# A three-layer graph attention kernel in fp32: gamma and beta of the first norm folded into W1, early loads in another order and place, the hidden split read from zt, and E turned through another PSUM bank

## The reference

```python
h = relu(layernorm(x))                          # no gamma, beta
for l in range(3):
    si = h @ attn_w[l, :d];  sj = h @ attn_w[l, d:]
    s = leaky_relu(si[:, :, None] + sj[:, None, :] + attn_b[l], 0.2)
    attn = softmax(where(adj + eye > 0, s, -inf))
    y = layernorm(h + attn @ h) * g1[l] + beta1[l]
    ff = gelu(y @ W1[l] + b1[l]) @ W2[l] + b2[l]    # W1: 256 x 1024
    h = layernorm(y + ff) * g2[l] + beta2[l]
return x + h
```

## Time and profile before

| what | value |
|---|---|
| median of 3 runs | 1242.52 us (1242.37 to 1242.93) |
| profiled execution, its own time | 1241.6 us |
| its span, first to last instruction | 1239.8 us |
| busy: PE, DVE, ACT, POOL | 1196.4, 1075.9, 920.0, 677.4 us |
| chain that ended last | PE 95%, DVE 3%, SP's queue 1%, DMA 1% |
| mean granted TensorE clock | 0.998 |
| POOL L487 (h_gamma), 128x512 | 96 times, mean 1298 ns |

### The profile page before, as it was taken

How to read it: one execution, slowest core, us unless ns; L and a number is a source line. 1 busy time by engine, 2 the same in 40 slices (tenths; PEclk the granted TensorE clock), 3 DMA queues, 4 the chain that set the end, 5 groups by cost and what they waited for, 6 DMA issues and landing times.

```text
span 1239.8 us, 23072 instructions
## 1 busy us (share of the span) xinstructions
PE 1196.4 (97%) x7509; PEld 1082.8 (87%) x7509; DVE 1075.9 (87%) x3568; ACT 920.0 (74%) x1754; POOL 677.4 (55%) x648
## 2 busy tenths in 40 slices
PE   2699999999999999999999999999999999999997
PEld 1589999998999999999999999999999999999996
DVE  5899889999998888899998888899989988888865
ACT  3786887678877776778778767777887777677752
POOL 1354455456755554456666545554666455545564
PEclk9999999999999999999999999999999999999999
DMA  7122322233332111222432122122432321122221
GB/s 256 38 77 73 99 70 60 77 94 112 103 103 88 50 44 52 85 71 85 129 114 92 43 59 70 44 69 78 125 115 80 100 60 43 44 69 61 78 89 48
DMA packets 109620, 100.57 MB, mean 81 GB/s; under 512 B 12952, under 2 KB 95932, under 8 KB 109500
## 3 DMA queue, kind: packets, MB, share of 16 engines
q1 hardware_dynamic: 109500, 99.10, 26.3%
HBM read 66.47 MB, written 32.60 MB: 80 GB/s over the span
## 4 chain that ended last, share of the span: by engine, by line
PE 95%; DVE 3%; SPq 1%; DMA 1%; issue 0%; POOL 0%; ACT 0%; DVEq 0%; POOLq 0%
PE acc L1073 44%; PE hbank L1058 42%; PE mix L1087 7%; PE mix L1112 2%; DMA adji<-in_adj_dram 1%; DVE xs L757 0%; DVE junk L694 0%; DVE st L603 0%; DVE st L764 0%; SPq L313 0%; PE util L1104 0%; SPq L332 0%; DVE sc L729 0%; POOL rstd L467 0%; DVE hid_lo L615 0%
## 5 line engine op out<-in xcount | busy, mean ns | idle before, releaser
L1073 PE MATMUL acc<-w2hi,hid_hi 128*128 128x256 f32 x1536 | 442.2, 288 | 0.0
L1073 PE MATMUL acc<-w2hi,hid_lo 128*128 128x256 f32 x1536 | 434.5, 283 | 0.0
L1073 PE MATMUL acc<-w2lo,hid_hi 128*128 128x256 f32 x1536 | 434.4, 283 | 0.0
L912 ACT ACTIVATE hbank<-hbank,vec 128x512 f32<-128x512 f32 x384 | 255.4, 665 | 178.1 <-PE hbank L1058 167.0
L1058 PE MATMUL hbank<-ht_hi,w1hi 128*128 128x512 f32 x768 | 305.7, 398 | 3.6 <-DVE hid_lo L615 2.0
L1058 PE MATMUL hbank<-ht_lo,w1hi 128*128 128x512 f32 x768 | 300.7, 392 | 0.0
L1073 PEld LDWEIGHTS acc<-w2lo,hid_hi 128*128 128x128 f32 x1536 | 294.0, 191 | 6.9
L1073 PEld LDWEIGHTS acc<-w2hi,hid_hi 128*128 128x128 f32 x1536 | 293.9, 191 | 6.9
L1058 PE MATMUL hbank<-ht_hi,w1lo 128*128 128x512 f32 x768 | 299.3, 390 | 0.0
L615 DVE TENSOR_TENSOR hid_lo<-hbank,hid_hi 128x512 fp32r<-128x512 f32 x384 | 259.9, 677 | 39.4 <-ACT hid_hi L918 39.4
L1073 PEld LDWEIGHTS acc<-w2hi,hid_lo 128*128 128x128 f32 x1536 | 293.9, 191 | 0.0
(11 more groups left out here) (80 smaller groups left out, 1708.4 us busy)
## 6 DMA issues: line engine op xcount, KB each, us to landing
z_dram<-tz SPq DMA_DIRECT2D x46, 512.0 KB, 2.6
zt<-z_dram SPq DMA_DIRECT2D x184, 128.0 KB, 2.8
sj_bc<-sj_dram SPq DMA_DIRECT2D x47, 256.0 KB, 3.9
xraw<-in_x_dram SPq DMA_DIRECT2D x16, 512.0 KB, 4.1
out_dram<-xout SPq DMA_DIRECT2D x32, 256.0 KB, 3.0
xres<-in_x_dram SPq DMA_DIRECT2D x15, 512.0 KB, 5.0
xout<-in_L_gnn_W_dram SPq DMA_DIRECT2D x10, 512.0 KB, 5.5
adji<-in_adj_dram SPq DMA_DIRECT2D x16, 256.0 KB, 3.5
```

Of the source, the lines that this page charges most:

```text
L912: act.activation(hbank[k % HB][:], hbank[k % HB][:], ACT.Gelu, bias=b1c(i.l, c)).then_inc(gelu_n, 1)
L1073: mm = pe.matmul(to, v[:, k % HID, of_g], w[:, i.l, c], start=c == 0 and n == 0 and g % HG == 0, stop=c == C - 1 and n == 2, skip_group_ch ...
```

## The change

1. **Fold.** W1 is scaled by gamma when it is rounded and split (ACT and DVE, one instruction each as before), and beta is taken into the bias: PE multiplies each staged half of W1 with beta (`beta_rows`, eight one-column fp32 matmuls into util) and DVE adds (`beta_sums`) into b1f. `h_out` is gone: `h_high` and `h_low` read util (i0, i1) or zt directly. gamma and beta stay in POOL's rows for the residual.
2. **E through util.** `e_turn` writes util instead of mix[0] and waits for util's last reader, not for `attend` of the item before.
3. **Loads.** EARLY = 2: x of i1, i2 go to hb[:, 0] and zt, adj of i1, i2 to two halves of tz. SP issues x1, adj1, W halves 0 to 3, b2, gamma and beta rows, x2, adj2, half 4, adj3, x3, and the rest behind. A half whose staging buffer held W1 also waits for its `beta_rows`.
4. **Order.** All five lists are written anew.

```diff
-EARLY = 1
+EARLY = 2
+        b1f = sb("b1f", [P, L, C])
-        early = [hb[:, i] for i in range(EARLY)]
-        def b1c(l, c): return vec[:, l * C + c:l * C + c + 1]
+        early = [hb[:, 0], zt[:].rearrange("p m a g t -> p (m a g t)").rearrange("p (g d) -> p g d", g=GG)]
+        early_adj = tz[:].bitcast(I32).rearrange("p c g t -> p (c g t)").rearrange("p (i g j) -> p i g j", i=EARLY, g=GG)
+        def b1c(l, c): return b1f[:, l, c:c + 1]
...
             def load_adj(i):
-                wait(sp, edge_n, i.g)
-                sp.dma_start(adji[:], group(adj, i.g)).then_inc(adj_in, 16)
+                t, arrived, _ = adj_of(i)
+                if arrived is adj_in:
+                    wait(sp, edge_n, 1 if i.q == 1 + EARLY else i.g)
+                sp.dma_start(t, group(adj, i.g)).then_inc(arrived, 16)
...
                 if n >= 4:
-                    sp.wait_ge(w_lo, n - 1 if n >= 6 else n - 3)
+                    before = n - 2 if n >= 6 else n - 4
+                    sp.wait_ge(w_lo, before + 1)
+                    if halves[before][1] == 0:
+                        sp.wait_ge(wbeta_n, KD * halves[before][0] + halves[before][2] + 1)
...
             def split_weights(n):
+                    if w == 0:
+                        dve.scalar_tensor_tensor(out=half_on_chip(1, l, w, h), in0=half_staged(n), scalar=g1c(l, h),
+                                                 in1=half_on_chip(0, l, w, h).bitcast(F32),
+                                                 op0=ALU.mult, op1=ALU.subtract).then_inc(w_lo, 1)
...
+            def beta_sums(n):
+                if 0 <= n < len(halves) and halves[n][1] == 0:
+                    l, _, h = halves[n]
+                    done = KD * l + h
+                    dve.wait_ge(wbeta_n, done + 1)
...
+                    dve.tensor_tensor(b1f[:, l], util[:, 0:C], before, ALU.add).then_inc(b1f_n, 1)
...
             def h_low(i, m):
                 dve.wait_ge(hthi_n, KD * i.q + m + 1)
-                dve.tensor_tensor(ht_lo[:, i.q % 2, m], util[:], ht_hi[:, i.q % 2, m].bitcast(F32),
-                                  ALU.subtract).then_inc(htlo_n, 1)
+                if i.q < BY_PE:
+                    dve.tensor_tensor(ht_lo[:, i.q % 2, m], util[:], ht_hi[:, i.q % 2, m].bitcast(F32),
+                                      ALU.subtract).then_inc(htlo_n, 1)
+                else:
+                    dve.tensor_tensor(by_block(ht_lo[:, i.q % 2, m]), zt[:, m],
+                                      by_block(ht_hi[:, i.q % 2, m].bitcast(F32)), ALU.subtract).then_inc(htlo_n, 1)
...
+                    if w == 0:
+                        act.activation(half_on_chip(0, l, w, h), half_staged(n), ACT.Copy, scale=g1c(l, h)).then_inc(w_hi, 1)
...
             def gelu(i, c):
+                if c == 0:
+                    act.wait_ge(b1f_n, KD * (i.l + 1))
...
             def e_turn(i):
-                wait(pe, y1_n, GG * (i.q - 1) + HG)
-                turned = mix[0][:].rearrange("p g d -> p (g d)")
+                wait_util_read()
+                read["e"] += 1
...
+            def beta_rows(n):
+                if 0 <= n < len(halves) and halves[n][1] == 0:
...
+                    wait_util_read()
+                    read["b"] += 1
+                    for c in range(C):
+                        mm = pe.matmul(util[:, c:c + 1], half_staged(n)[:, c * P:(c + 1) * P], beta1c(l, h),
+                                       start=c == 0, stop=True, skip_group_check=True)
+                    mm.then_inc(wbeta_n, 1)
```

More of the change, by code:

```diff
@@ L842, in _ @@
+            masked(i0)
+            minus_max(i0)
+            split_weights(0)
+            penalty(i1)
             input_moments(i1)
-            i_dots(i0)
-            split_weights(0)
+            attend(i0, 0)
+            attend(i0, 1)
             input_shift(i1)
-            masked(i0)
-            penalty(i1)
-            minus_max(i0)
+            moments1(i0)
+            beta_sums(0)
+            split_weights(1)
             j_dots(i1)
+            beta_sums(1)
+            norm1(i0)
@@ L850, in _ @@
+            h_low(i0, 0)
+            split_weights(2)
+            penalty(i2)
+            h_low(i0, 1)
             input_moments(i2)
             i_dots(i1)
-            split_weights(1)
-            attend(i0, 0)
-            split_weights(2)
             input_shift(i2)
-            masked(i1)
-            attend(i0, 1)
-            minus_max(i1)
-            moments1(i0)
-            j_dots(i2)
-            penalty(i2)
-            norm1(i0)
-            h_low(i0, 0)
-            attend(i1, 0)
@@ L865, in _ @@
-            i_dots(i2)
-            h_low(i0, 1)
-            attend(i1, 1)
-            masked(i2)
-            moments1(i1)
-            minus_max(i2)
             split_weights(3)
             low(i0, 0)
-            norm1(i1)
+            masked(i1)
             input_moments(i3)
+            minus_max(i1)
+            j_dots(i2)
             low(i0, 1)
             low(i0, 2)
-            penalty(i3)
+            low(i0, 3)
             input_shift(i3)
-            low(i0, 3)
-            attend(i2, 0)
+            i_dots(i2)
@@ L881, in _ @@
+            j_dots(i3)
+            masked(i2)
             low(i0, 4)
-            attend(i2, 1)
-            h_low(i1, 0)
-            moments1(i2)
-            j_dots(i3)
+            attend(i1, 0)
+            minus_max(i2)
+            attend(i1, 1)
+            moments1(i1)
+            i_dots(i3)
+            norm1(i1)
             low(i0, 5)
             low(i0, 6)
+            h_low(i1, 0)
+            penalty(i3)
+            split_weights(4)
+            attend(i2, 0)
             h_low(i1, 1)
@@ L889, in _ @@
             low(i0, 7)
-            i_dots(i3)
-            norm1(i2)
-            masked(i3)
-            split_weights(4)
-            low(i1, 0)
-            turn_z(i2)
-            low(i1, 1)
+            attend(i2, 1)
+            masked(i3)
+            moments1(i2)
+            residual(i0, 0)
+            residual(i0, 1)
+            low(i1, 0)
+            norm1(i2)
+            beta_sums(4)
             for s in range(1, ITEMS + 3):
```

318 lines of the change are left out of this document (171 added, 147 removed).

## The result

The changed kernel takes 1246.16 us (median of 8 runs, 1244.51 to 1247.92) against 1242.40 us for the kernel before (8 runs, 1242.18 to 1242.93). The ratio is 1.0029, 95% interval 1.0018 to 1.0040: 0.3% slower, where 1238.5 us was forecast and 1242.8 us was the top of the range. The profiled execution took 1244.51 us, with a span of 1242.7 us.

The account below looks back on a forecast made before the run. PE was taken as the bound, unbroken from 155 to 1000 us; an earlier first slot (-7.6) plus added beta matmuls (+3.6) gave -4.0 us, so 1237.6 profiled and 1238.5 us median, range 1234.8 to 1242.8.

Parts of the forecast that it names:

- Part 1: Start of item 0: exponentials begin at 14.8 instead of 24.45, ffn1(i0,0) at 33.1 instead of 46.59, 13.5 us sooner.
- Part 2: From 33.1 to the first slot, set by DVE's list: slot at 71.4 against 78.70, gain taken as 7.6 us.
- rival (a): No change: one-column matmuls cost what aggregation's do, or PE stays slow through two ffn1; 1242 to 1244; chance 0.18.
- the answer to it: Argument against (a)'s slow PE pace, 2 us over two ffn1: DVE sets that stretch, not PE.
- Part 3: W1 times beta added to PE: 0.9 us a half, 3.6 us in all for halves 4, 5, 8 and 9.
- the 1.2 named as a sign of being wrong: Forecast's own test: wrong if a group of eight one-column matmuls takes over 1.2 us.
- my upper end, 7.3: Cost in us of the one-column matmuls in the unbroken stretch at aggregation's 0.205 each.
- 3 to 4 were named: Sign of being right: PE busy 3 to 4 us more in all.
- Part 4: Edits counted at nothing: fewer ScalarE passes, scaled W1 split, E through util, W1 loads waiting for beta matmuls, later turn_z.
- the slot: New slot order: PE never waits, with margins of 0.3 to 0.9 us, so no stall is counted.
- Rival (b): Slower: a wait each slot, at minus_max 23 us (1261), or by the SBUF rule at h_low up to 18; chance 0.14.
- the margin: Slack of 0.9 us at h_low in the slot; a loss of 0.7 beside GpSimd's add_input was taken to fit.

Follow-up runs that it names:

- e2: Changed kernel without W1 times beta in layers 1 and 2 (halves 4, 5, 8, 9 left out): 1241.99 us, 0.9993 of the kernel before.
- h1: Changed kernel's loads and opening before the old slots, no one-column matmuls, gamma and beta one ScalarE pass, E through its old bank: 1239.77 us.
- e1: Changed kernel without W1 times beta in all three layers (bias is b1 alone): 1239.63 us, 0.9978 of the kernel before.
- e4: Kernel before with the second item's adjacency loaded early and the first row maxima ahead of the second item's penalty: 1239.80 us.
- e6: Changed kernel with each group of eight one-column matmuls issued twice: 1269.01 us, 1.0209 of the kernel before.
- c0_after: Changed kernel run again without edit: 1245.81 us, 1.0024 of the kernel before.
- h1_again: h1 run once more without edit: 1239.92 us, 0.9976 of the kernel before.
- h3: h1 with low(i1,1), residual(i0,0), minus_max(i3) and residual(i0,1) moved ahead of norm1(i2) and turn_z(i2) on VectorE: 1240.41 us.

## Why the prediction was wrong

By its own steps, for the profiled execution: 1237.6 forecast, 1244.51 measured, 6.9 too low; the median stands 1.65 above the profiled execution instead of 0.9, which is the last 0.75.

**Part 1, 1.8 us off.** The exponentials began at 14.86 (14.8 forecast) and the adjacency group caused no wait: right. ffn1(i0,0) came at 34.91, not 33.1. Two causes. The b1f sum ahead of norm1(i0) waits 1.21 us for half 1, which took 3.48 us at the lower clock level where half 0 took 1.84; I had written that they run while PE idles, and had looked only at PE, not at who waits for them. And norm1(i0) takes 2.32 us, not the 1.37 of the earlier trace rows, since GpSimd now does h_gamma(i0,0) beside it:

```profile
28.89 1.27 POOL L501 TENSOR_TENSOR hb<-xs,ln_rows 128x512 f32<-128x512 f32 x1 [1.99 <-DVE xs L809]
```

Only the last of its four parts is longer, 1.35 us instead of 0.41, and it ends at 30.31, just behind the addition. I had looked for such a meeting at the instructions with two SBUF inputs. This one is a TENSOR_SCALAR with one tensor input. The Trainium skill (SBUF — State Buffer, Who interferes with whom) lists tensor_scalar among the operations that can contend with GpSimd for a port, if its operands allow a faster mode; the 2.32 against 1.37 agree with it, and so does norm2 above.

**Part 2, nearly right.** From 34.91 to 72.62 are 37.7 us, where 33.1 to 71.4 were 38.3 walked. The first slot's place was 1.2 us late; the gain 6.1 instead of 7.6 (I had added 0.3 to the walk). PE did stay at the slow pace through two ffn1 and into the third, as rival (a) says, and it cost nothing, as the answer to it says: see e2. The further 1.2 us of the second clock fall stand in some executions and were in no step.

**Part 3, the failing step: 3.7 us.** I took 0.09 us for a one-column matmul and called a group 0.9; it is 1.82, over the 1.2 named as a sign of being wrong, and four halves 7.3. The nearest row was chosen by the stationary's size and the column count. It was a transposition, and the trace of before held what tells the two apart. PE's rows by line in the kernel before, for 48 items:

```profile
L1087 PE MATMUL mix<-xs,ET x384: 377/379/797, 27.3 to 1174.4; 128*128 128x256 f32 x192
```

```profile
L1112 PE MATMUL mix<-ident,sc x192: 270/272/476, 25.0 to 1171.4; 128*128 128x128 f32 x192
```

The code issues four matmuls an item in either: 192. The transposition has one row each, the fp32 matmul two. An fp32 matmul is two rows of the trace, which I call passes, and the one-column ones are sixteen rows a half, 0.115 us each. I had divided the aggregation's 1.64 us by eight rows and called 0.205 one matmul; it is half of one, so that even my upper end, 7.3, was an upper end of nothing: one matmul of the aggregation is 0.41, and 32 of them 13. That the measured sum equals it is chance. PE's extra 14.2 us, where 3 to 4 were named, are these 7.3, the 5.3 of halves 0 and 1, which the sum had at nothing, and 1.6 of the slots.

**Part 4 and the slot, 1.6 us.** No stall came: after 90 us PE waits 0.4 us in all. Rival (b) and its 18 or 23 us did not happen. h_low from zt met GpSimd's add_input in 13 of 92 calls and took 0.89 us there against 0.68, within the margin:

```profile
L819 DVE TENSOR_TENSOR ht_lo<-zt,ht_hi 128x512 fp32r<-128x512 f32 x92 | 62.0, 714 | 0.5 <-ACT ht_hi L984 0.5
```

But an order of PE's work without a stall is not yet free, and I had put it at nothing. The old slot has ffn1 in four runs of 1, 2, 3 and 2, the new one in six; three ffn1 in a row take 4.11 us, one alone between ffn2's 1.38 to 1.39. 0.036 us a slot over 44 slots is 1.6 us. That this is the alternation is argued from these spacings; that it lies in the new slots is shown by h1.

**Sum:** 1.5 (opening) + 3.7 (matmuls) + 1.6 (slots) = 6.8 of 6.9. It adds lengths along PE's work. Taken out in e1, W1 times beta gives back 6.1 us, not 7.3: half 4 is nearly hidden, halves 0 and 1 are not. Of the rivals (a) had the sign of the matmuls' part and no more; none was slower for the right reason. Starting the first slot sooner worked in kind, 6.1 us for 7.6. But in h1, where nothing is added to PE, 2.8 us of it are left in the median, and e4 has the same 2.8 from two small edits.

## What to carry to other kernels

Where one engine is busy without a gap, a change that adds work to it must be costed by that engine's own rows for the same operation, counted: rows in the trace against instructions in the code tells how many passes one has. Work put into another engine's idle time is hidden only if nobody waits for its result; look up the reader too. And measure the parts of a bundle apart: here the two smallest edits reach the whole gain, the new slots only cost, and the fold pays about what it earns. A clock column is read from the first record of the clock on; before it, the spacing of like matmuls tells the level.

## What the runs showed of the hardware

- An fp32 matmul with a 128x128 stationary and one column costs 0.23 us (two rows of 0.115), 1.82 to 1.84 us for eight at the full clock level and 3.41 to 3.54 at the lower; with 256 columns 0.41. A transposition with 128 columns costs 0.09.
- TensorE's granted clock can fall to its lower level though its records leave no gap: in e6 with or behind 32 one-column passes in a row at four places, for 3 to 7 us, at a cost of 1.5 to 3.1 us in a slot beyond the passes' own.
- Behind a wait of some 2 us in the opening it falls in some executions and not in others (c0_after against the first execution, h1_again against h1; also e2 and h3), 1.2 us or more each time. This is one source of the wider spread of all versions with the new opening (2.4 to 4.8 us, and 6.3 in e6's four runs, against 0.7 to 2.7 for the kernel before); whether it is the only one is open, since only the profiled executions show it.
- The clock column shows 1.00 in e1 where the trace has no record of the clock yet, though its matmuls, 0.43 us apart, run at the lower level's pace.
- Four VectorE tensor_scalar parts took 2.32 us instead of 1.37 beside a GpSimd addition of 1.27; norm2's take 689 ns on average instead of 428.
